# The three 16-head attentions of a four-layer kernel: 64x64 tiles for scores and masks, three bank pairs in turn, small jobs in even rounds, stacks loaded in halves

## The reference

```python
q = q.reshape(B, T, H, D).transpose(0, 2, 1, 3)      # k and v likewise
att = jnp.einsum('bhqd,bhkd->bhqk', q, k) * (1.0 / math.sqrt(D))
att = att + jnp.where(rel <= 0, slopes * rel, -jnp.inf)[None]   # layer 1; causal mask alone in 2 and 3
att = jax.nn.softmax(att, axis=-1)
y = jnp.einsum('bhqk,bhkd->bhqd', att, v).transpose(0, 2, 1, 3).reshape(B, T, C)
return y @ w_proj.T
```

## Time and profile before

| | us |
|---|---|
| median of three runs | 2914.24 |
| the profiled execution | 2911.34 |
| its span | 2909.5 |
| TensorE matmul busy | 2305.2 (79%) |
| TensorE weight load busy | 1476.4 (51%) |
| VectorE busy | 1535.6 (53%) |
| ScalarE busy | 1138.6 (39%) |
| GpSimd busy | 637.8 (22%) |
| keyed masks, matmuls (L1176, 1536) | 157.7 |
| masked maxima (L1282, L1284, 1536) | 541.5 |

### The profile page before, as it was taken

The page is one execution under the profiler, slowest core; times in us unless marked ns, Lnnn a source line. Parts: engine busy times, 40 slices in busy tenths (PEclk is TensorE's granted clock), DMA queues, the critical chain, the costliest instruction groups (busy, mean ns, idle before and its releaser), DMA issues. The chain is left out here.

```text
span 2909.5 us, 54198 instructions
## 1 busy us (share of the span) xinstructions
PE 2305.2 (79%) x18107; PEld 1476.4 (51%) x18108; DVE 1535.6 (53%) x5386; ACT 1138.6 (39%) x1810; POOL 637.8 (22%) x689
## 2 busy tenths in 40 slices
PE   4487999997699999784888828447888866999997
PEld 1133777773267777431444416324554313777775
DVE  4635666635466665435677313147775245565663
ACT  5623554433244544333555402133554340233333
POOL 0204434300244342002010040421110012221210
PEclk8796999998899999896999869767999865899999
DMA  2000000000000000001222140202221002333330
GB/s 109 0 0 1 1 1 0 0 1 0 0 1 2 0 0 1 1 4 45 70 80 67 55 150 0 62 28 81 73 74 33 0 33 90 92 111 91 91 110 30
DMA packets 81241, 115.82 MB, mean 40 GB/s; under 512 B 10352, under 2 KB 67184, under 8 KB 77720
## 3 DMA queue, kind: packets, MB, share of 16 engines
q1 hardware_dynamic: 79024, 109.48, 12.4%
q0 software_dynamic: 2048, 4.20, 0.5%
HBM read 69.70 MB, written 42.86 MB: 39 GB/s over the span
## 5 line engine op out<-in xcount | busy, mean ns | idle before, releaser
L1240 ACT ACTIVATE at_pr<-ps 128x768 f32<-128x768 f32 x384 | 312.1, 813 | 505.7 <-PE ps L1176 505.7
L1282 DVE CUSTOM_DVE_ANT_0 at_junk<-ps,conf 128x128 f32<-128x128 f32 x768 | 220.1, 287 | 235.7 <-PE ps L1158 216.0
L1284 DVE CUSTOM_DVE_ANT_0 at_junk<-ps,conf 128x256 f32<-128x256 f32 x768 | 321.4, 419 | 0.0
L1158 PE MATMUL ps<-at_ks,at_qs 40*128 40x128 f32 (+5 forms) x2048 | 223.0, 321 | 70.7 <-DVE at_m L1284 26.9
L1170 PE MATMUL ps<-at_qs,at_ks 41*128 41x256 f32 (+5 forms) x2048 | 199.5, 294 | 58.2 <-DMA at_qs<-at_ml 28.4
L693 POOL TENSOR_TENSOR la_tc<-la_ta,la_tb 128x512 f32<-128x512 f32 x128 | 162.3, 1268 | 354.6 <-DVE la_tb L959 354.6
L710 PE MATMUL ps<-w_l0f,la_hs 128*128 128x512 f32 x256 | 152.5, 680 | 54.4 <-POOL la_hs L675 36.3
L1170 PEld LDWEIGHTS ps<-at_qs,at_ks 41*128 41x128 f32 (+2 forms) x2048 | 140.9, 145 | 105.9 <-ACT at_pr L1240 53.5
L860 ACT ACTIVATE la_pr<-ps 128x640 f32<-128x640 f32 x128 | 90.2, 705 | 265.8 <-PE ps L762 265.4
L1191 PE MATMUL ps<-at_pr,at_v 128*32 128x256 f32 (+1 forms) x3072 | 175.8, 341 | 16.4 <-issue 15.7
L1158 PEld LDWEIGHTS ps<-at_ks,at_qs 40*128 40x128 f32 (+2 forms) x2048 | 104.9, 151 | 160.3 <-DVE at_m L1284 59.2
(11 more groups left out here) (308 smaller groups left out, 4995.6 us busy)
## 6 DMA issues: line engine op xcount, KB each, us to landing
scratch_latent<-at_parts SPq DMA_DIRECT2D x32, 640.0 KB, 4.8
at_qs<-scratch_latent SPq DMA_DIRECT2D x32, 320.0 KB
at_ks<-scratch_latent SPq DMA_DIRECT2D x32, 320.0 KB
scratch_alibi<-at_parts SPq DMA_DIRECT2D x32, 192.0 KB, 2.3
at_ks<-scratch_alibi SPq DMA_DIRECT2D x192, 32.0 KB
scratch_rope<-at_parts SPq DMA_DIRECT2D x32, 192.0 KB, 2.3
at_ks<-scratch_rope SPq DMA_DIRECT2D x192, 32.0 KB
moe_weights<-in_moe SPq DMA_DIRECT2D x1, 4096.0 KB, 20.7
```

The lines of the kernel that those rows point to most:

```text
L1158: m = nc.tensor.matmul(o[:, cols:cols + keys], q[:, block_q:block_q + P], kk[:, 0:keys], start=True, stop=True)
L1240: nc.scalar.activation(pr[:, p % RING, :, :], ps[:, 6:8, 0:384], ACT.Exp, scale=scale).then_inc(s.at_prob, 1)
L1282: nc.vector.tensor_tensor_reduce(junk[:, x % 2, e, 0:P], ps[:, m + e, 0:P], k.cf("late")[:, P:2 * P], 1.0, BIG, ALU.add, ALU.max, m2[:, r, ...
L1284: last_max = nc.vector.tensor_tensor_reduce(junk[:, x % 2, e, P:3 * P], ps[:, m + e, P:3 * P], k.cf("late"), 1.0, BIG, ALU.add, ALU.max, m ...
```

## The change

- Scores and keyed scores are issued as tiles of 64x64: the stationary operand is 64 columns wide and goes to PSUM partitions 0 to 63 or 64 to 127. Eight matmuls a round instead of four, in each pass.
- Both passes get their mask by `quarter_masks`, four 64x64 matmuls that each write two blocks of 128 columns. VectorE's maximum becomes two plain reductions with negation; the constant `late` goes, two crossed copies of the masks come.
- In layers 1 and 2 scores and keyed scores take three bank pairs (2 to 7) in turn.
- Small jobs move to even rounds: `shifts` from 1 to 0, `value_rows` from 5 to 2, `turn` from 7 to 6, layer 1's product from 3 to 4, layer 3's five products from rounds 2 to 6 to pairs in rounds 2, 4 and 6. Some PSUM copies change between ScalarE and VectorE.
- Each row's stack loads are split in two halves (rounds 0 to 3, rounds 4 to 7) with a semaphore each. SP's order in a step is now: first half of row `i - 1`, shift DMAs of row `i - 3`, second half of row `i - 1`, stores of row `i`.

```diff
+    crossed = [(name + "_x", np.roll(a, P // 2, 0)) for name, a in (("causal_q", causal), ("causal_k", causal.T))]
-            ("late", np.concatenate([np.zeros((P, P)), BIG * np.triu(np.ones((P, P)), 1)], 1))]
...
+        def score_bank(n, x):
+            return 2 + 2 * ((n + 2 * x) % 3) if deep else 2
+        def keyed_bank(n, x):
+            return 2 + 2 * ((n + 2 * x + 1) % 3) if deep else 6
+        def until(i, x, first, back):
+            u = HP * i + x - first - back + 1
+            return HP * row0 + (min(max(u, 0), HP * B) if isinstance(i, int) else u)
+        def scored_until(i, x, back):
+            return until(i, x, 2 * HP, back)
+        def keyed_until(i, x, back):
+            return until(i, x, 3 * HP + KEY_LAG, back)
...
+            def load_half(i, n, g):
+                r, nr = i - 1, (n - 1) % slots
+                sem = (s.at_stacked0, s.at_stacked1)[g]
+                if g == 0:
+                    sp.wait_ge(s.at_scratch, 32 * (row0 + r + 1))
+                at_least(sp, sem, 16 * (sd0 + nst * r))
+                if live(i, 1 + slots):
+                    at_least(sp, s.at_keyed, HP * (row0 + r - slots) + HP // 2 * (g + 1))
+                for dst, src in a.stack_loads(nr, g):
+                    sp.dma_start(dst, src).then_inc(sem, 16)
             def step(i, n):
+                if live(i, 1):
+                    load_half(i, n, 0)
                 if live(i, 3):
                     sp.wait_ge(s.at_mt, row0 + i - 2)
...
                 if live(i, 1):
-                    for dst, src in a.stack_loads(nr):
-                        sp.dma_start(dst, src).then_inc(s.at_stacked, 16)
+                    load_half(i, n, 1)
...
+            def quarter_masks(bank, name):
+                for c in range(2):
+                    for e in range(2):
+                        r = slice(64 * e, 64 * e + 64)
+                        rows = k.cb(name if c == e else name + "_x")[r, :]
+                        out = ps[64 * c:64 * c + 64, bank + e, 0:3 * P].rearrange("p (b t) -> p b t", t=P)[:, 0:3:2, :]
+                        m = nc.tensor.matmul(out, k.cb("ident", 64 * e, 64)[r, :], rows.unsqueeze(1).to_broadcast([64, 2, P]),
+                                             start=False, stop=True, skip_group_check=True)
+                return m
             def scores(i, n, x):
-                    pe.wait_ge(s.at_stacked, 16 * (sd0 + nst * (i + 1)))
-                at_least(pe, s.at_max, u - deep + 1)
+                    pe.wait_ge(s.at_stacked0, 16 * (sd0 + nst * (i - 1)))
+                if x == HP // 2:
+                    pe.wait_ge(s.at_stacked1, 16 * (sd0 + nst * (i - 1)))
+                if deep:
+                    at_least(pe, s.at_prob, keyed_until(i, x, 2))
+                    if isinstance(i, int):
+                        at_least(pe, s.at_max, scored_until(i, x, 3))
+                else:
+                    at_least(pe, s.at_max, scored_until(i, x, 1))
                 for block_q, cols, keys in ((0, 0, P), (P, P, 2 * P)):
-                    for e in range(2):
...
+                    for c in range(2):
+                        for e in range(2):
+                            q, kk = stacks((n - 2) % slots, x, e, stack_rows)
+                            nc.tensor.matmul(ps[64 * c:64 * c + 64, bank + e, cols:cols + keys],
+                                             q[:, block_q + 64 * c:block_q + 64 * c + 64], kk[:, 0:keys],
+                                             start=(cols == 0), stop=False, skip_group_check=True)
+                quarter_masks(bank, "causal_q").then_inc(s.at_score, 1)
...
+                if deep:                                  # keyed, in the same 64x64 form
+                    at_least(pe, s.at_max, scored_until(i, x, 1))
+                    if isinstance(i, int):
+                        at_least(pe, s.at_prob, keyed_until(i, x, 3))
+                else:
+                    at_least(pe, s.at_prob, keyed_until(i, x, 1))
...
-                            nc.vector.tensor_tensor_reduce(junk[...], ps[:, m + e, 0:P], k.cf("late")[:, P:2 * P], 1.0, BIG, ...)
-                            last_max = nc.vector.tensor_tensor_reduce(junk[...], ps[:, m + e, P:3 * P], k.cf("late"), 1.0, BIG, ...)
+                        nc.vector.tensor_reduce(m2[:, r, 0, x:16:8], ps[:, at:at + 2, 0:128], AX.X, ALU.max, negate=True)
+                        nc.vector.tensor_reduce(m2[:, r, 1, x:16:8], ps[:, at:at + 2, 128:384], AX.X, ALU.max, negate=True
+                                                ).then_inc(s.at_max, 1)
...
-    def stack_loads(n):
-        loads = []
+    def stack_loads(n, g):
+        loads, w = [], HP // 2 * L
         for e in range(2):
-            cols = slice(e * HP * L, (e + 1) * HP * L)
+            cols = slice((2 * e + g) * w, (2 * e + g + 1) * w)
             q, kk = (scr[n, j].rearrange("s (d h) t -> (s d) (h t)", h=H16)[:, cols] for j in range(2))
-            at = lambda stack, lo, hi: stack[64 * e + lo:64 * e + hi, n, :]
+            at = lambda stack, lo, hi: stack[64 * e + lo:64 * e + hi, n, g * w:(g + 1) * w]
             loads += [(at(a.Qs, 0, 24), q[0:24]), (at(a.Qs, 24, 40), q[0:16]), (at(a.Qs, 40, 48), q[0:8])]
             loads += [(at(a.Ks, 8 * j, 8 * j + 8), kk[8 * m:8 * m + 8]) for j, m in enumerate((0, 0, 0, 1, 1, 2))]
...
-    PRODUCTS = {2: 0, 3: 1, 4: 2, 5: 3, 6: 4}
+    PRODUCTS = {2: (0, 1), 4: (2, 3), 6: (4,)}
```

More of the change, by code:

```diff
@@ L1103, in shifts, with turn @@
                 for q in range(2):
[L1104 to L1110 removed]
+                    m = nc.tensor.matmul(ps[:, 0, L + q * P:L + (q + 1) * P], xv[:, n, q * P:(q + 1) * P], value_w,
+                                         start=True, stop=True)
+                m.then_inc(s.at_vprod, 1)
+            def turn(i):
+                bank_free(i, 6)
+                pe.wait_ge(s.at_raw, row0 + i - 3)
+                if deep:
                     at_least(pe, s.at_used, rd0 + rounds * done(i, 0))
@@ L1113, in value_rows @@
                     at_least(pe, s.at_stored, row0 + done(i, 5))
-                pe.nop(nofuse=True)
-                for q in range(2):
-                    m = nc.tensor.matmul(ps[:, 0, q * P:(q + 1) * P], xv[:, n, q * P:(q + 1) * P], value_w,
-                                         start=True, stop=True)
-                m.then_inc(s.at_vprod, 1)
-            def turn(i):
-                earlier(i, 7)
-                pe.wait_ge(s.at_raw, row0 + i - 3)
-                at_least(pe, s.at_vread, row0 + done(i, VALUE_ROW))
+                    at_least(pe, s.at_vread, row0 + done(i, VALUE_ROW))
                 pe.nop(nofuse=True)
@@ L1160, in scores @@
-                m.then_inc(s.at_score, 1)
-            def keyed(i, n, x):
-                u = HP * (row0 + i) + x
-                if x == 0:
-                    pe.wait_ge(s.at_mrow, 16 * (md0 + nm * (i + 1)))
-                at_least(pe, s.at_prob, u)
-                for keys, cols, first in ((0, 0, 0), (P, 2 * P, P)):
-                    for e in range(2):
-                        q, kk = stacks(n, x, e, last)
-                        nc.tensor.matmul(ps[:, 6 + e, cols:cols + L - first], kk[:, keys:keys + P], q[:, first:L],
-                                         start=(cols == 0), stop=False, skip_group_check=True)
@@ L1173, in keyed_masks @@
-            def keyed_masks():
-                for e in range(2):
-                    for cols in (0, 2 * P):
-                        m = nc.tensor.matmul(ps[:, 6 + e, cols:cols + P], k.cb("ident"), k.cb("causal_k"), start=False,
-                                             stop=(cols > 0), skip_group_check=True)
-                m.then_inc(s.at_keyed, 1)
+                    pe.wait_ge(s.at_stacked0, 16 * (sd0 + nst * (i - 1)))
+                if x == HP // 2:
+                    pe.wait_ge(s.at_stacked1, 16 * (sd0 + nst * (i - 1)))
@@ new lines, in scores @@
+                quarter_masks(bank, "causal_q").then_inc(s.at_score, 1)
+            def keyed(i, n, x):
+                row, p = 3 + (x < KEY_LAG), (x - KEY_LAG) % HP
+                if p == 0:
+                    pe.wait_ge(s.at_mrow, 16 * (md0 + nm * (i - row + 1)))
+                if deep:
+                    at_least(pe, s.at_max, scored_until(i, x, 1))
[3 more added lines that the diff above has]
+                    at_least(pe, s.at_prob, keyed_until(i, x, 1))
+                pe.nop(nofuse=True)
+                bank = keyed_bank(n, x)
+                for keys, cols, first in ((0, 0, 0), (P, 2 * P, P)):
+                    for c in range(2):
+                        for e in range(2):
+                            q, kk = stacks((n - row) % slots, p, e, last)
+                            nc.tensor.matmul(ps[64 * c:64 * c + 64, bank + e, cols:cols + L - first],
+                                             kk[:, keys + 64 * c:keys + 64 * c + 64], q[:, first:L],
+                                             start=(cols == 0), stop=False, skip_group_check=True)
```

(13 more changed lines are left out.)

152 lines of the change are left out of this document (73 added, 79 removed).

## The result

Over four runs each the changed kernel has a median of 3110.46 us (3101.38 to 3116.43), the kernel before 2913.47 (2911.65 to 2918.39). The ratio is 1.0671, 95% interval 1.0638 to 1.0704. The forecast was 3052, its range ended at 3105. The profiled execution of the changed kernel took 3114.84 us, its span 3113.0.

A forecast was written before the change was run, and what follows sets the result against it. It took waits between engines, a circle through SP's loads and stores, to bound the first two attentions; 2911.3 + 75 + 75 + 9 - 8 - 12 = 3050, stated as 3052 us for the median, range 2975 to 3105.

The forecast's parts named there:

- The circle: First two attentions: first half, shift DMAs to keyed scores, parts, stores, next first half; rows of 21.5 and 22.5 us.
- 6.45 + 2.87 us: SP's part of a row in the first two attentions: first half's loads 6.45, stores to next load 2.87 us.
- Rival 2: A load's price lies in its bytes or overlaps, so the kernel gets faster, 2855 us at 0.05 us a load; chance 8%.
- Rival 5: Halves do what they are for: scores start on half a stack, loads hide under a longer row, no change; chance 2%.
- C: First two attentions, keyed scores to parts ready: 6.6 and 7.6 us warm, plus 1.7 for the cold clock.
- cold surcharge: First two attentions: after TensorE's idle stop the clock falls to 0.50, adding 1.7 us a row between keyed scores and parts.
- rival 1: The clock holds, or idle time is spread over the row; rows of 19.8 and 20.8 us, total 3006; chance 20%.
- Steps 1 and 2: First two stages' start, without maxima DMAs: 18 more loads a step cost 0 to 12.4 us a stage, taken as +4.5.
- Third attention, -8: Fewer tiling pauses against waits for VectorE's maximum: a gain of 0.5 us a row, -8 us, bounds -20 and +14.
- Rival 3: Column halves of a row tile run in turn: +164 us in the third stage, total 3220; chance 7%.
- rival 4: Third stage: TensorE's sequencer cannot issue 418 matmuls a row at 60 ns; +14 instead of -8, total 3074; chance 5%.
- -12 in the tails: Last steps of the first two stages, without loads: about 28 rounds each gain 0.2 us, -6 us a stage.

The follow-up runs named there:

- halves_behind: The changed kernel with both halves of each row's loads (36) issued behind the shift rows; 2975.28 us, ratio 1.0216.
- before_halves: The kernel before with only the loads in halves and in the new order; 3085.51 us, ratio 1.0594.
- halves_full: The changed kernel, halves kept, with quarter tiles put together into 128-row tiles and full mask matmuls; 3165.07 us, ratio 1.0824.
- warm: The changed kernel with seven extra matmuls a row before the wait for shift rows in the first two attentions; 3121.83 us, ratio 1.0722.
- warm4: The changed kernel with four extra matmuls a row before the wait for shift rows in the first two attentions; 3097.97 us, ratio 1.0645.
- whole_behind: The changed kernel with whole stack loads (18 a row, 4 in the third attention) behind the shift rows, as before; 2931.37 us, ratio 1.0067.
- lone_products: whole_behind with projections back in their old rounds (round 3 in the first attention, one a round in the third); 2904.89 us, ratio 0.9984.
- steps_alone: The kernel before with three bank pairs and even steps; whole loads, 128-row tiles, keyed masks by one 256-column matmul a bank; 2929.39 us, ratio 1.0068.
- product_early: The changed kernel with the first attention's projection back in round 3 instead of round 4; 3087.13 us, ratio 1.0587.
- whole_ahead: The changed kernel with whole loads (18 a row), all ahead of the shift rows; 3370.81 us, ratio 1.1574.
- full_tiles: whole_behind with quarter tiles put together into 128-row tiles and full mask matmuls; 2974.23 us, ratio 1.0191.

## Why the prediction was wrong in size and right in kind

The circle and the clock were right. The step that failed is the price of SP's commands in it, 6.45 + 2.87 us a row, which measured 10.5; it makes 31 us. Besides, the gain of 8 us in the third attention was a loss of 14. Term by term:

- **36 loads at 0.36 us, by command and not by bytes:** right; 18 half loads took 6.2 us undisturbed. Rival 2 fell with it, halves_behind shows the price.
- **The circle:** right, in place and parts. before_halves has nearly the whole loss. Rival 5 fell as well.
- **The failing term: "6.45 (first half) ... 2.87".** Both were single undisturbed samples from the kernel before, in which SP waits for others and a long command is made up for. As means they are 6.8 and 3.7, 1.2 us a row more, +31 us over 26 rows. About 0.7 us of it goes when the quarter tiles go (halves_full, 9.74 and 9.80), and before_halves, without them too, has 9.89 and 10.08. So 0.4 to 0.7 us belongs to the quarter tiles; that their fetches do it rests on the count of long commands. The rest, about half a microsecond, has no cause that a run shows. From the shift commands to the keyed scores it was 4.10 and 4.02 us instead of 3.9, another +4.
- **C:** 8.3 and 9.3 forecast, 7.78 and 9.13 measured (to the stores); -9 us over both stages. The cold surcharge of 1.7 was right in the first attention and 1.1 to 1.7 in the second (warm, warm4), so rival 1, no clock drop, fell. The warm part was half a microsecond too long in the first attention.
- **The old rows:** I subtracted single rows, 15.7 and 16.7 us. Over the same 13 distances between stores that the circle governs, the kernel before has 16.08 and 16.48, the changed kernel 22.37 and 23.65. That is -5 and +3 us against what I subtracted, so these samples did no harm. The thirteen rows grew by 82 and 93 us where I had 75 each.
- **Steps 1 and 2, "+4.5 each":** the two first distances grew by 12.9 us in the first attention (20.2 to 33.1) and by 7.3 in the second (24.1 to 31.4), together +11 over my term. In the first SP had no waits to hide the 36 more loads in, which is the upper end of the 0 to 12.4 that I had allowed. From a stage's last stores to its end the changed kernel was 10.2 and 2.4 us shorter, together the -12 that I had.
- **Third attention, -8 (bounds -20 and +14): failed in sign.** By differences of profiled stages: pairs of projections +8.6 (whole_behind to lone_products, 496.8 to 488.2), halves +3.0 (whole_behind to after), and tiles, masks and reductions +2.4 (before to lone_products) where I had a gain. In these 2.4 are two stops at the loop's end, 3.1 and 2.7 us, so without the stops I get a gain of 3.4. I had weighed the empty odd rounds but not the fuller even ones, where VectorE's two rotations hold up the maxima. The pause ahead of the mask weights did go (44.4 to 1.3 us).
- **Quarters side by side:** right; 16 keyed matmuls on four tiles span 0.83 us, as 8 did in the earlier trace rows. Rival 3 fell:

```profile
2774.59 0.83 PE L1227 MATMUL ps<-at_qs,at_ks 41*64 41x256 f32 x16
```

- **Sequencer rate (rival 4):** lone_products issues the changed kernel's matmuls at 26.05 us a row of the third attention, before's 258 took 25.96; steps_alone, with the 128-row tiles, took 26.81 and whole_behind, with the quarters, 26.55. No limit shows. The Trainium skill (TensorE: Matmul & The Clock Gate, "Wait — 56ns, not 53.3ns?"), from which I had estimated 25.9 us, is not contradicted, and does not explain the 26.92.
- **Tiles and banks covered in the first two stages, -12 in the tails:** right in size. lone_products, too, is shorter there: its first two stages are 7.3 and 5.2 us shorter than before, and all of that lies behind the last store.
- **"The other edits at nothing":** wrong in one point that I had inside C without seeing its price: the projection's move is worth 20 us in the first attention (product_early).

Together, against the forecast of 3050 for the profiled execution: +11 and +24 in the first two stages, +22 in the third, +7 scatter elsewhere, 3114.8.

What stays open: why SP's commands take longer when instructions are fetched for, as far as the count shows, other engines; the trace doesn't name the engine of a packet. Nor is it shown what TensorE waits for at the loop's end. A version that shortens the loop without changing the tiles was not tried; it is the test for both, and lone_products has 20.7 us of such stops to win. In the second attention the tiles and the banks win back 14 us under the halves (481.1 to 467.4); which of them, no run tells.

## What to carry to other kernels

Draw the circle before splitting a transfer: count the commands that the issuing queue gets, and for each command that is moved ahead of another, list the waits in front of it; those waits move too (whole_ahead lost 15% by one of them). A term that enters a circle needs the mean over a stage and not one clean row, since in a circle every irregularity is paid. When means are compared, take the same steps in both kernels: the rows at a pipeline's start are shorter than those in the middle. Jobs gathered into even rounds are free only where no other job's result is waited for in the same round.

## What the runs showed of the hardware

- From one command of SP to the next it took 0.34 to 0.37 us (medians) for loads of 16, 32 and 320 KB alike, 0.7 us for the shift rows.
- With the quarter tiles there were 174 to 187 instruction packets of 16.4 KB (queue q8) where there were 92. The Trainium skill (Runtime: NRT & Kernel Launch, "Terms") says that each engine's instruction memory is refilled in blocks of 16 KiB; the packets' size agrees. In the same kernels TensorE stopped for 4.7 to 5.2 us where the loop goes back to its start, in the first two attentions (until 1476.0 us in lone_products, 1530.8 in the changed kernel), and for 2.6 to 3.1 in the third (whole_behind, lone_products and the changed kernel). SP commands that were long were longer by 1 us on average and up to 2.3 us, and each stood beside a packet.
- Four 64x64 mask matmuls of 256 columns in different quarters went side by side: in 768 groups of four they kept TensorE busy 245 us, two full ones in their place 311 (full_tiles).
- In the changed kernel TensorE idled 4.6 to 7 us in most rows and the granted clock was at 1.2 GHz for 6.8 us around the end of it, at 1.7 us a row in the first attention; from 1385 to 1660 us there were 13 such stretches in the changed kernel and 6 with four matmuls in the stop.
